# Causal zeroes of transposed attention scores: by mask matmuls before the exponential, or by GpSimd after it

## The reference

```python
attn = jnp.einsum('nhqd,nhkd->nhqk', q, k) * scale
causal = jnp.tril(jnp.ones((t, t), dtype=bool))
attn = jnp.where(causal, attn, -jnp.inf)
attn = jax.nn.softmax(attn, axis=-1)
out = jnp.einsum('nhqk,nhkd->nhqd', attn, v)
```

## Time and profile before

| | |
|---|---|
| median of three runs | 759.89 us |
| profiled execution, span from first to last instruction | 757.7 us |
| what the median has beyond that span | 2.2 us |
| PE busy | 660.7 us, 87% |
| DVE busy | 514.1 us, 68% |
| ACT busy | 342.2 us, 45% |
| POOL busy | 151.8 us, 20% |
| attention of layer 0, with ST units | about 78 to 246 us |
| attention of layer 1, with ST units | about 507 to 688 us |

### The profile page before, as it was taken

One profiled execution on the slowest core, in us unless ns is written; L12 is line 12 of the kernel. 1 busy time (PEld: TensorE's weight loads), 2 busy tenths in 40 slices (PEclk: granted clock), 3 DMA queues, 4 the chain that ended last, 5 costly groups with the idle time before them and its releaser, 6 DMA issues.

```text
span 757.7 us, 13009 instructions
## 1 busy us (share of the span) xinstructions
PE 660.7 (87%) x5007; PEld 464.5 (61%) x5007; DVE 514.1 (68%) x1313; ACT 342.2 (45%) x472; POOL 151.8 (20%) x145
## 2 busy tenths in 40 slices
PE   1478889999989899999999998999989899998664
PEld 0333556565655699898998785775555655555443
DVE  6578776777743536658537467777786778666993
ACT  1110566656575444433444432335546455674221
POOL 5301010100011010010021301302203010345764
PEclk9995999999999999999999999999999999999985
DMA  5405876454320000000000200211211211000000
GB/s 152 126 22 147 173 218 132 85 141 75 66 55 14 1 1 1 1 1 1 1 1 1 63 1 12 75 23 28 83 42 27 65 45 35 25 12 1 14 15 28
DMA packets 29325, 38.07 MB, mean 50 GB/s; under 512 B 3719, under 2 KB 23185, under 8 KB 29265
## 3 DMA queue, kind: packets, MB, share of 16 engines
q1 hardware_dynamic: 29265, 37.25, 20.3%
HBM read 26.33 MB, written 10.88 MB: 49 GB/s over the span
## 4 chain that ended last, share of the span: by engine, by line
PE 64%; DVE 25%; issue 5%; ACT 3%; POOL 1%; DMA 0%; POOLq 0%; DVEq 0%; ACTq 0%
PE ps L989 14%; PE ps L486 9%; PE ps L444 7%; DVE mx L663 6%; PE ps L465 6%; PE ps L979 4%; PE ps L512 3%; PE ps L981 3%; PE ps L980 3%; DVE xn L926 3%; PE ps L447 2%; ACT pT L557 1%; PE ps L494 1%; PE ps L469 1%; DVE x L1063 1%
## 5 line engine op out<-in xcount | busy, mean ns | idle before, releaser
L663 DVE TENSOR_REDUCE mx<-ps 128x1 f32<-128x384 f32 (+3 forms) x352 | 215.5, 637 | 72.5 <-PE ps L447 70.4
L557 ACT ACTIVATE pT<-ps 128x1024 f32<-128x1024 f32 x160 | 162.1, 1023 | 86.9 <-PE ps L469 71.9
L1024 ACT ACTIVATE pT<-ps,b1c 128x512 f32<-128x512 f32 x128 | 87.8, 687 | 129.6 <-PE ps L981 128.7
L989 PEld LDWEIGHTS ps<-w_sb,pT 128*128 128x128 f32 x1024 | 132.2, 191 | 11.8 <-issue 1.3
L989 PE MATMUL ps<-w_sb,pT 128*128 128x128 f32 x1024 | 135.5, 275 | 0.0
L447 PE MATMUL ps<-mask_qk,identb 128*128 128x128 bf16 (+2 forms) x352 | 90.2, 256 | 0.0
L444 PE MATMUL ps<-stA 96*128 96x128 bf16 (+3 forms) x256 | 69.6, 332 | 19.2 <-DVE mx L663 14.3
L486 PE MATMUL ps<-pT,vA 128*32 128x512 f32 (+3 forms) x1024 | 77.9, 439 | 0.7 <-ACT pT L557 0.7
L1063 DVE SCALAR_TENSOR_TENSOR x<-ps,comb,x 128x128 f32<-128x128 f32 x128 | 36.0, 344 | 58.4 <-PE ps L989 58.3
L444 PE MATMUL ps<-kA,stA 96*128 96x128 bf16 (+3 forms) x256 | 63.7, 304 | 12.8 <-DVE mx L663 11.6
L979 PE MATMUL ps<-x_hi,w_hi 128*128 128x512 f32 x128 | 62.9, 491 | 1.2 <-DVE w_lo L1045 1.0
(11 more groups left out here) (232 smaller groups left out, 964.1 us busy)
## 6 DMA issues: line engine op xcount, KB each, us to landing
stA<-stack_scratch SPq DMA_DIRECT2D x48, 192.0 KB, 3.4
stB<-stack_scratch SPq DMA_DIRECT2D x48, 192.0 KB, 4.5
stack_scratch<-part SPq DMA_DIRECT2D x12, 384.0 KB, 3.2
w_sb<-in_L_ffn_W_dram SPq DMA_DIRECT2D x16, 256.0 KB, 5.6
stack_scratch<-part SPq DMA_DIRECT2D x12, 256.0 KB, 3.1
stack_scratch<-part SPq DMA_DIRECT2D x12, 128.0 KB, 3.1
x<-in_L_attn_z_dram SPq DMA_DIRECT2D x4, 256.0 KB, 4.4
out_dram<-x SPq DMA_DIRECT2D x4, 256.0 KB, 2.3
```

The lines of the kernel that those rows point to most:

```text
L557: act.activation(dst_, src, ACT.Exp, scale=SCALE).then_inc(a["ex"], 1)
L663: nc.vector.tensor_reduce(mx[:, g % 2, qb, heads[0]:heads[0] + nh], ps[:, S_BANK[n % 2], 0:nh * w].rearrange("p (h k) -> p h k", h=nh), AX ...
L989: last = pe.matmul(ps[:, ST_BANK[1] + m % 2, f * P:(f + 1) * P], hT[:, (m % 2) * FC + c, f * P:(f + 1) * P], w2_sb[:, e, c, :], start=(c = ...
L1024: act.activation(hT[:, (m % 2) * FC + f, :], ps[:, ST_BANK[0] + n % 2, :], ACT.Gelu, bias=b1c[:, e * FC + f:e * FC + f + 1]).then_inc(M["g ...
```

## The change

The five ST units keep the matmuls of line 465 and lose all mask matmuls; the last matmul into each block now closes it (`stop`). ScalarE takes the exponential of unmasked scores. Behind each exponential GpSimd sets to 0 what lies below the diagonal of the 128x128 blocks on it, in place in `pT`, with `affine_select`: two operations for each of units 0 to 3 (one over two blocks, one over one block) and one for unit 4 (four blocks). PV now waits for a new semaphore `cut`, which the last of them raises, in place of `ex`. `mask_kq` is no longer made, so the counts of `made` are lower by one. The S units keep their masks.

```diff
@@ attention_tensor, ST
-                    pe.matmul(o, kk[:, kb * P:(kb + 1) * P], stB[:, 0, h, kb * P:T], start=(at % 512 == 0), stop=False)
-
-                if u < HG:
-                    pe.matmul(ps[:, base, 0:P], identb[:], mask_kq[:], start=False, stop=True)
-                    last = pe.matmul(ps[:, base + 1, :].rearrange("p (a c) -> p a c", a=NB)[:, 0:4:3, :], identb[:],
-                                     mask_kq[:].unsqueeze(1).broadcast_to([P, 2, P]), start=False, stop=True)
-                else:
-                    for c in range(2):
-                        last = pe.matmul(ps[:, base + c, :].rearrange("p (h k) -> p h k", h=2)[:, :, 0:P], identb[:],
-                                         mask_kq[:].unsqueeze(1).broadcast_to([P, 2, P]), start=False, stop=True)
+                    last = pe.matmul(o, kk[:, kb * P:(kb + 1) * P], stB[:, 0, h, kb * P:T], start=(at % 512 == 0),
+                                     stop=(kb in (0, 3) or at % 512 > 0))
+
                 last.then_inc(a["st"], 1)
             elif name == "PV":
-                pe.wait_ge(a["ex"], (i + 1) * NV)
+                pe.wait_ge(a["cut"], i + 1)
@@ attention_gpsimd
+        def below_diagonal(blocks, n):
+
+            return nc.gpsimd.affine_select(blocks, blocks, compare_op=ALU.is_ge, fill=0.0, base=0,
+                                           pattern=[[0, n], [1, P]], channel_multiplier=-1)
...
+            elif name == "ST":
+
+                pool.wait_ge(a["ex"], i * NV + u + 1)
+                if u < HG:
+                    two_ = pT[:, g % 2, u, 0:1024].rearrange("p (a c) -> p a c", a=2)[:, :, 0:P]
+                    below_diagonal(two_, 2)
+                    below_diagonal(pT[:, g % 2, u:u + 1, KB_AT[3][0]:KB_AT[3][0] + P], 1)
+                else:
+                    below_diagonal(pT[:, g % 2, :, KB_AT[2][0]:KB_AT[2][0] + P], HG).then_inc(a["cut"], 1)
```

More of the change, by code:

```diff
@@ L256, in network @@
         mask_qk = sb("mask_qk", [P, P], BF16)
-        mask_kq = sb("mask_kq", [P, P], BF16)
         ones = sb("ones", [P, P])
@@ L374, in network @@
         both = ("xnT q k v qhi khi qrest krest qmid kmid split vraw va store "
-                "sc maxd mt negm mpart mstore st ex pv oTs ot on ont onTs wo xdone").split()
+                "sc maxd mt negm mpart mstore st ex cut pv oTs ot on ont onTs wo xdone").split()
         rotary = "qs ks qf kf qsum ksum kacc kparts rotq rotk bias".split()
@@ L895, in setup_gpsimd @@
                 nc.gpsimd.memset(vA[:].rearrange("p n h c -> p (n h c)"), 0.0).then_inc(made, 1)
-                pool.wait_ge(made, 8)
+                pool.wait_ge(made, 7)
                 nc.gpsimd.memset(vA[:, :, :, DK], 1.0).then_inc(made, 1)
@@ L1321, in _ @@
             sp.dma_start(cent_sb[:], cent).then_inc(ld_e, 16)
-            sp.wait_ge(made, 7)
+            sp.wait_ge(made, 6)
             for c, w in ((0, wg), (1, wu)):
@@ L1341, in _ @@
         def _(pe):
-            pe.wait_ge(made, 3)
+            pe.wait_ge(made, 2)
             free = [None]
@@ L1390, in _ @@
             nc.gpsimd.tensor_copy(identb[:], ident[:]).then_inc(made, 1)
-            for m, step, mul in ((mask_qk, -1, 1), (mask_kq, 1, -1)):
+            for m, step, mul in ((mask_qk, -1, 1),):
                 link(nc.gpsimd, nc.gpsimd.memset(m[:], 0.0))
@@ L1398, in _ @@
             nc.gpsimd.memset(fill[:], 1.0).then_inc(made, 1)
-            pool.wait_ge(made, 7)
+            pool.wait_ge(made, 6)
             for stage, *step in order:
@@ L1408, in _ @@
                     fp4_gpsimd(pool, *step)
-MADE = 11
+MADE = 10
 _INS = ["L0_attn_z", "L0_attn_Wqkv", "L0_attn_Wout", "L0_ffn_centroids", "L0_ffn_Wp", "L0_ffn_bp", "L0_ffn_W1",
```

## The result

| kernel | median us (lowest to highest, runs) | ratio to before, 95% interval |
|---|---|---|
| before, same chip | 760.63 (759.38 to 762.92, 20) | 1 |
| changed | 765.12 (759.19 to 767.54, 20) | 1.0046 [1.0031, 1.0061] |

What follows compares the result with a forecast made beforehand. TensorE was fullest, but the chain alternates between TensorE's masks and VectorE's maxima and MP; GpSimd was not the bound. -14.3 + 5.0 + 0.8 + 0.8 + 2.2 + 4.2 = -1.3 us gave 758.6 us, range 749 to 767.

Steps and rivals of the forecast that it cites:

- Masks, -14.3: Both attentions: removing mask matmuls on the chain, 18.3 us at most, gains 14.3 us after discounts.
- TensorE's time was not worth it: Rival: only half the chain's masks come off, 9 us not 14.3, 764 us; chance 0.27 shared with held operations.
- Select prices: GpSimd's affine_select: 0.29 us for 128 columns, 0.41 for 256, 0.64 for 512, interpolated from its copy.
- Held MP, 5.0: VectorE's MP operations wait while selects run: 0.3 us in 16 groups, all paid by TensorE, 5.0 us.
- ScalarE behind GpSimd, 0.8: Layer 1: four GpSimd sums that ScalarE waits for stand behind selects, 0.2 us each, 0.8 us.
- norms and key parts: VectorE's normalisations and parts of the key meet selects in a few places: 0.8 us.
- End of layer 0, 2.2: Selects queue behind GpSimd's root, PV 1.5 us later, and VectorE's routing is held: 2.2 us in all.
- of layer 1, 4.2: Last selects queue behind QH on GpSimd, last PV 3.9 us later, 0.3 for held roundings: 4.2 us.
- Sum: Whole kernel: gain and costs add to -1.3 us, giving 758.6 us, within the 0.2% a measurement can tell.
- what would have shown it wrong: Signs: selects twice as long, PV waiting in mid-stage, MP staying at 0.17 us, middles gaining much other than 2.5 us.
- held operations of the routing: End of layer 0: VectorE's short routing operations held by selects of seven units, within that end's 2.2 us.
- the 4.0 us of discount: Taken off the 18.3 us of masks: 2.4 for unit 0's pairs ahead of MP, 1.6 for the two tails.

Runs made afterwards that it cites:

- e1: Changed kernel with neither mask matmuls nor selects in the ST units, causal zeroes left out: 750.46 us, 0.9852 of the kernel before.
- e5: Changed kernel with ST unit 0 of every group masked by matmuls again, without selects: 763.53 us, 1.0039 of the kernel before.
- e2: Kernel before with all mask matmuls kept and all selects added: 776.02 us, 1.0189 of the kernel before.
- e8: Kernel before with all mask matmuls kept, selects added only in each layer's last group: 772.19 us, 1.0128 of the kernel before.
- e4: Changed kernel with 15 extra matmuls on TensorE ahead of each layer's last PV, to keep it busy: 763.04 us, 1.0021 of the kernel before.
- e12: e8 with 11 (layer 0) and 17 (layer 1) extra matmuls in the last PV's wait: 768.84 us, 1.0104 of the kernel before.
- e3: Changed kernel with each layer's last group masked by matmuls again, without selects: 756.77 us, 0.9942 of the kernel before.
- e10: Changed kernel with each layer's last two groups masked by matmuls again, without selects: 757.43 us, 0.9952 of the kernel before.
- e6: Changed kernel with unit 0 of every group and each layer's last two groups masked by matmuls, without selects: 757.5 us, 0.9948 of the kernel before.
- e9: Changed kernel with GpSimd's second QH product issued behind the last group's selects: 762.54 us, 1.0023 of the kernel before; repeated, 762.37 us, 1.0015.
- e7: Changed kernel run again unaltered: 765.18 us, 1.0052 of the kernel before.

## Why the prediction was wrong, step by step

- **Masks, -14.3: the first term that failed; mis-sized, 11.3 measured (e1).** The pairs on the chain were counted rightly (18.3 us), but a chain read before the change doesn't say what is next behind it. Behind it stood VectorE: TensorE's wait for MP grew by 3.2 us and its wait for the maxima by 4.6. The middles gave 3.4 and 5.3 us where some 5.6 each were counted, the ends 1.1 where 3.2 were (e1's profiled execution). The rival "TensorE's time was not worth it" was right in kind; it said 9, and that its 764 us lie near the measured 765.1 is luck.
- **Select prices: right** to 0.01 us (interpolated 0.41 and 0.64, measured 0.411 and 0.634).
- **Held MP, 5.0: mechanism right, and the size nearly so.** (16 x 0.3 is 4.8; the sum took 5.0.) MP is 4.4 us longer in all, by 0.18 us in 24 groups rather than 0.3 in 16, and TensorE waits for it 3.8 us longer than in e1 (21.3 and 17.5). That the kernel's time pays all of it was not shown: e5 took it away together with the selects of unit 0 and gained nothing that can be told.
- **ScalarE behind GpSimd, 0.8: not seen** (16.4 and 16.5 us). With this, held MP and 0.8 for norms and key parts, the middles' cost was put at 6.6; e2 and e8 leave 4.7.
- **End of layer 0, 2.2, and of layer 1, 4.2: the second term that failed, and the step left out of it.** Together 6.4, measured 9.7 (e8). The queues were named rightly. The delay of the last PV is near in layer 1, 3.6 us for 3.9 (exponentials done at 686.93, PV at 690.56), and too small in layer 0, 2.8 for 1.5. Left out was what TensorE is after such a wait. Its clock is half: each of the two PVs takes 2.14 us longer, and the transposes behind the second 0.45. What this costs in all is known only roughly. The ratios of e4 give 1.9 us of the change, those of e12 1.8 of e8. The traces give 2.6 behind the PV of layer 1; in layer 0, from the PV to the 17th H, e4 is 2.3 us shorter than the changed kernel (35.1 and 37.4), but e12 only 0.2 shorter than e8.
- **Sum.** -14.3 + 6.6 + 6.4 = -1.3 became -11.3 + 4.7 + 9.7 = +3.1, and the measured change is +3.5. Masks +3.0, middles -1.9, ends +3.3. Either the first or the last alone turns the sign of -1.3; the middle one is within the noise of two runs subtracted. That the middles came out near the forecast is partly luck, since there the masks brought less and the selects cost less.

Of what would have shown it wrong, one point came: PV does wait before the last group, 1.15 us at 680.71. Its selects stand behind an earlier QH, which ends at 677.64.

Two things stay open. The experts' first 16 groups take 30.8 us from the first H before and 33.0 after, and 32.0 to 32.9 in e3, e10, e12 and e4, which have no half clock at the PV. This goes with a fall of the clock between 253 and 262 us, while these groups run: e1, e6, e8 and e9 do not have it there and need 30.4 to 31.4 us. Its cause wasn't found. And of the ends' 9.7 us the delays of the two PVs (2.8 + 3.6 in the changed kernel, 1.8 + 4.3 in e8) and the clock (1.9) explain some 8; the rest lies within the interval of e8, and held operations of the routing, which the forecast put at 0.7, were not measured.

The best versions are e3, e10 and e6, 0.6% to 0.5% under the kernel before and not told apart. e3 is the simplest: selects everywhere, matmul masks in the last group of each layer, where GpSimd has other work and nothing stands behind PV to fill the wait.

## What to carry to other kernels

Work moved to an idle engine can be cheap in the middle of a pipelined stage and dear at its end (here some 4.7 us for 270 selects, and 9.7 for 18): price the last group by itself, with the queue it finds on its new engine. Where the change makes TensorE wait for some microseconds, add to the wait what its next matmuls cost at half clock, and try keeping it busy or leaving the last group as it was. Take a gain read off the chain at less than its length: of the 18.3 us of masks on it 11.3 were got here, and the 4.0 us of discount in the forecast were too few, since the engine saved waited longer for the next one.

## What the runs showed of the hardware

- TensorE's clock fell at nearly every long wait of a last PV. Waits of 3.49 and 3.45 us (changed kernel), 3.49 and 3.20 (e7), 3.94 (e8, layer 1), 3.27 (e2, layer 0) and 3.35 (e5, layer 0) were followed by 32 matmuls in 4.49 to 4.50 us, in place of 2.36; waits of 2.38 (e8, layer 0), 3.49 (e9, layer 0) and 3.76 (e5, layer 1) by 4.05, 3.68 and 4.02 us, partly at full clock. One of 3.07 us (e2, layer 1) left it full. So the length of the wait alone does not tell it. With 15 matmuls of 512 columns in the wait (e4) it stayed full in both layers, and so it did with 11 and 17 (e12).
- `affine_select` in place on fp32: 292 ns for 128 columns, 411 for 256, 634 for 512.
- In the group shown a select of 0.41 us made a VectorE operation of MP 0.15 us longer, and the one of 0.29 us behind it the next operation 0.04: 0.65 us of selects lengthen a group's four operations by some 0.2.
